# One transposition and one correction product for both tiles of a pair, and bias rows by label

## The reference, cut to what matters

```python
x = x + conv(x masked by length, one SSM kernel per channel)       # L0, a causal convolution, masked again
x = x + einsum('bct,bcd->bdt', x, weights[cond])                    # L1, mixing of channels, 16 sets
x = x + x @ base_weight.T + base_bias + (x @ A[id].T) @ Bw[id].T    # L2, 32 adapters of rank 16
x = x + x @ W.T + (x @ lora_A[label]) @ lora_B_w.T * 0.5            # L3, 5 labelers of rank 32
```

## Time and profile before

| | |
|---|---|
| time, median of 3 runs | 1446.25 us (1444.93 to 1446.51) |
| profiled execution: its own time | 1442.18 us |
| its span, first to last instruction | 1440.4 us |
| granted TensorE clock | 1.000 |
| PE busy | 1429.8 us, 99% |
| DVE busy | 1127.4 us, 78% |
| ACT busy | 612.7 us, 43% |
| POOL busy | 100.9 us, 7% |
| DMA | 271.94 MB, mean 189 GB/s |

### The profile page before, as it was taken

The page is one execution under the profiler, slowest core; times in us unless marked ns, Lnnn a source line. Parts: engine busy times, 40 slices in busy tenths (PEclk is TensorE's granted clock), DMA queues, the critical chain, the costliest instruction groups (busy, mean ns, idle before and its releaser), DMA issues.

```text
span 1440.4 us, 31629 instructions
## 1 busy us (share of the span) xinstructions
PE 1429.8 (99%) x9368; PEld 1329.8 (92%) x9368; DVE 1127.4 (78%) x2288; ACT 612.7 (43%) x1217; POOL 100.9 (7%) x193
## 2 busy tenths in 40 slices
PE   9999999999999999999999999999999999999998
PEld 7888899999999999999999999999999999999997
DVE  7975498888888887777777777787777777778775
ACT  4331376666666663333433433433343343343331
POOL 2322100000000002000000000000000000000000
PEclk9999999999999999999999999999999999999999
DMA  8033288888888886564564565556556556555652
GB/s 315 1 129 79 76 283 272 276 277 272 277 268 276 273 274 183 170 203 148 166 200 146 162 197 163 153 182 190 153 162 204 146 161 203 153 153 190 182 154 81
DMA packets 117070, 271.94 MB, mean 189 GB/s; under 512 B 24173, under 2 KB 60401, under 8 KB 114381
## 3 DMA queue, kind: packets, MB, share of 16 engines
q1 hardware_dynamic: 107048, 237.86, 54.1%
q10 hardware_dynamic: 9990, 33.68, 5.8%
HBM read 198.59 MB, written 72.85 MB: 188 GB/s over the span
## 4 chain that ended last, share of the span: by engine, by line
PE 95%; DVE 2%; DMA 2%; SPq 0%; issue 0%; POOL 0%; ACT 0%; DVEq 0%; POOLq 0%; ACTq 0%
PE ps L796 18%; PE ps L789 17%; PE ps L1704 14%; PE ps L788 12%; PE ps L769 8%; PE ps L1603 7%; PE ps L1715 6%; PE ps L805 4%; PE ps L1695 3%; PE ps L1707 2%; PE ps L1589 1%; PE ps L780 1%; PE ps L1612 1%; DMA p<-in_L_cond_base_weight 1%; DMA out<-y_out 1%; PE ps L775 1%
## 5 line engine op out<-in xcount | busy, mean ns | idle before, releaser
L789 PE MATMUL ps<-weights,xa 128*128 128x352 f32 x1152 | 323.0, 322 | 0.0
L788 PE MATMUL ps<-weights,xa 128*128 128x256 f32 x1152 | 321.8, 281 | 0.5 <-ACT y_out L597 0.5
L796 PE MATMUL ps<-weights,xs 128*128 128x512 f32 x1152 | 291.2, 401 | 0.0
L796 PEld LDWEIGHTS ps<-weights,xs 128*128 128x128 f32 x1152 | 207.0, 189 | 40.4
L1704 PE MATMUL ps<-toep,ut 128*128 128x512 f32 (+2 forms) x1152 | 226.7, 342 | 0.0
L788 PEld LDWEIGHTS ps<-weights,xa 128*128 128x128 f32 x1152 | 217.3, 189 | 2.5 <-issue 1.1
L789 PEld LDWEIGHTS ps<-weights,xa 128*128 128x128 f32 x1152 | 216.2, 188 | 1.3
L1704 PEld LDWEIGHTS ps<-toep,ut 128*128 128x128 f32 x1152 | 194.3, 189 | 16.6
L568 ACT ACTIVATE a<-ps 128x512 f32<-128x512 f32 x128 | 76.7, 599 | 281.9 <-PE ps L769 281.2
L769 PE MATMUL ps<-m_gath,x_in 128*128 128x128 f32 x1024 | 134.6, 275 | 1.3 <-DVE x_in L660 1.3
L769 PEld LDWEIGHTS ps<-m_gath,x_in 128*128 128x128 f32 x1024 | 126.6, 191 | 4.0 <-DVE x_in L660 1.5
(11 more groups left out here) (227 smaller groups left out, 2255.3 us busy)
## 6 DMA issues: line engine op xcount, KB each, us to landing
xt<-in_xt SPq DMA_DIRECT2D x64, 512.0 KB, 5.7
x_d<-yo SPq DMA_DIRECT2D x64, 512.0 KB, 2.9
x_nat<-in_x SPq DMA_DIRECT2D x64, 512.0 KB, 3.8
lags<-kern_d SPq DMA_DIRECT2D x63, 512.0 KB, 5.0
x_in<-x_d SPq DMA_DIRECT2D x62, 512.0 KB
out<-y_out ACTq DMA_DIRECT2D x62, 512.0 KB, 5.8
stack<-b_d SPq DMA_DIRECT2D x130, 128.0 KB, 3.9
tab<-a_d SPq DMA_DIRECT2D x128, 128.0 KB, 2.1
```

The costliest lines, as they stand in the source:

```text
L788: mm(acc[:, left, 0:HALF], x_part, w[:, 0:HALF], start=start, stop=end, skip_group_check=True)
L789: ins = mm(acc[:, right, 0:HALF + KR], x_part, w[:, HALF:WIDE], start=start, stop=end, skip_group_check=True)
L796: ins = mm(acc[:, bank], operand[:, a, i, :], plain(i, b, m), start=opens and i == a == b == 0, stop=i == K4 - 1 and a == 1, skip_group_ch ...
```

## The change: what it does

- `hrow`, `hc` and `c_gath` exist once and hold both tiles: rows and columns 0 to 79 are tile 0, and from 80 on for tile 1 in part. One `turn` and one `adapters` product serve a pair. The high half of `hs[1]` and `stack[1]` stands in the upper rows.
- The bias is no longer part of `c_gath`. The bias row with the correction of a label is made beforehand for each of the 5 labels (`row_d`, 5 x 2 x 1024) and loaded into the stack by label: one more DMA per sample.
- SP reads all eight ids (adapter and label of four samples) before it waits for `p_done` and loads the stacks, then the eight ids of the next pair.
- `low_rank(0, 0)` goes behind M3; `adapters` goes behind quarter 1; on VectorE `h_stack` of both tiles goes behind L738.
- In the preparation the bias product goes from "c" to "a3b", "c" gets five one-column products and "row" two more wide ones.

```diff
     def load_stack(eng, v, a, l):
         for b in range(2):
             row = b * (R2 + R3)
+            high, low, bias = HIGH[v] + row, LOW[v] + row, LOW[v] + 2 * b
...
+            eng.dma_start(f(stack[v][bias:bias + 2, 1]), row_d[bass.ds(l[b], 1)].squeeze(0)).then_inc(stack_landed[v], 16)
...
         def load_c(v, a, l):
             for b in range(2):
...
-                sp.dma_start(c_gath[v][rows, H3], c_adapters[bass.ds(a[b], 1), :, cols].squeeze(0)).then_inc(c_landed[v], 16)
-                sp.dma_start(c_gath[v][KS + b:KS + b + 1, H3], c_d[AR:AR + 1, cols]).then_inc(c_landed[v], 16)
+                row = v * KS + b * (R2 + R3)
+                to = c_gath[row:row + R2, v * KS + R2:v * KS + R2 + R3]
+                sp.dma_start(to, c_adapters[bass.ds(a[b], 1), :, bass.ds(l[b] * R3, R3)].squeeze(0)).then_inc(c_landed[v], 16)
...
         def stacks(n):
...
+            a, l = [ids(sp, n, v, B) for v in range(2)], [ids(sp, n, v, 2 * B) for v in range(2)]
             sp.wait_ge(p_done, n)
             for v in range(2):
-                load_stack(sp, v, ids(sp, n, v, B))
+                load_stack(sp, v, a[v], l[v])
...
@@ VectorE, pair(n)
             dve.wait_ge(m2_done, n + 1)
             h_rows(n, 0)
-            h_columns(n, 0)
             if not last_one:
                 choose(n + 1, 1, 0)
             dve.wait_ge(m4_done, n + 1)
             h_rows(n, 1)
-            h_stack(n, 0)
-            h_columns(n, 1)
             if not last_one:
                 first_low(n + 1)
+            h_columns(n)
+            if not last_one:
                 choose(n + 1, 1, 1)
-            h_stack(n, 1)
             dve.wait_ge(m6_done, n + 1)
             dve.wait_ge(pair_sums, 2 * n + 2)
             tt(y_out[0][:, HB:T], y_out[1][:, HB:T], of_p, ALU.add).then_inc(u2_read, 1)
+            for v in range(2):
+                h_stack(n, v)
...
@@ TensorE, pair(n)
-            wide_product(xa22, M4, V_LEFT, V_RIGHT, FRONT, False)
-            turn(n, 0)
-            wide_product(xa22, M4, V_LEFT, V_RIGHT, BACK, False).then_inc(m4_done, 1)
-            adapters(n, 0)
+            wide_product(xa22, M4, V_LEFT, V_RIGHT, ALL, False).then_inc(m4_done, 1)
...
             plain_product(xs2, M6, P_BANK, FRONT, True)
-            turn(n, 1)
+            turn(n)
             plain_product(xs2, M6, P_BANK, BACK, False).then_inc(m6_done, 1)
-            pe.wait_ge(hs_lo, 2 * n + 1)
-            pe.wait_ge(stack_landed[0], 64 * n + 64)
...
-            low_rank(0, 0, PIECES_S).then_inc(lr11_done, 1)
-            adapters(n, 1)
             if not last_one:
                 quarter(n + 1, 1)
+            adapters(n)
             pe.wait_ge(s4_lo, n + 1)
             ready(pe, y12_added, n)
             plain_product(xs4, M3, Q_BANK, ALL, True)
+            pe.wait_ge(hs_lo, 2 * n + 1)
+            pe.wait_ge(stack_landed[0], 96 * n + 96)
...
+            low_rank(0, 0, PIECES_S).then_inc(lr11_done, 1)
             if not last_one:
                 quarter(n + 1, 2)
...
@@ preparation: VectorE, then TensorE
+            dve.wait_ge(in_b3, 16)
+            ts(b3n[B3_ROWS], b3n[B3_ROWS], 0.5, None, ALU.mult).then_inc(b3_scaled, 1)
             t = target("c")
             dve.wait_ge(job_done, done("c"))
+            nc.vector.tensor_copy(crt[B3_ROWS], t[0:R3, HB + LR:HB + LR + L3N]).then_inc(crt_ready, 1)
...
-            over_chunks(t[0:1, HB + LR:HB + 2 * LR], lambda c: bias_col[:, c:c + 1], lambda c: a3raw[:, c, :]).then_inc(job_done, 1)
+            for l in range(L3N):
+                ins = mm(t[0:R3, HB + LR + l:HB + LR + l + 1], c_row[:, l * R3:(l + 1) * R3], ones[0:1, 0:1], start=True, stop=True)
+            ins.then_inc(job_done, 1)
             t = job("row")
             pe.wait_ge(bias_ready, 1)
+            pe.wait_ge(b3_scaled, 1)
```

More of the change, by code:

```diff
@@ L106, in program @@
     bias_col, o = at("bias_col", [P, K8], F32, o)
-    ones, o = at("ones", [P, 1], F32, o)
+    ones, o = at("ones", [P, L3N], F32, o)
+    crt, o = at("crt", [P, L3N], F32, o)
     o = o_w[0]
@@ L135, in program @@
     c_row, o = at("c_row", [1, LR], F32, o)
+    b3n, _ = at("b3n", [P, T], F32, o_c - AR // P * 4 * T)
     assert o <= o_w[2]
@@ L229, in program @@
     m_gath = both("m_gath", [P, P])
-    hrow = both("hrow", [P, P])
+    hrow = place("hrow", [P, P])
     x_nat[1], o = at("x_nat1", [P, T], F32, o_rest + 4 * T + 4 * TFOLD)
@@ L362, in program @@
     PAIRS = TILES // 2
-    c_adapters = c_d[0:AR].rearrange("(a r) c -> a r c", r=R2)
+    c_adapters = c_d.rearrange("(a r) c -> a r c", r=R2)
     x1_rows = x1_d.rearrange("(n b) c t -> n (b c) t", b=2)
@@ L484, in dense_sync @@
         for v in range(2):
-            for to, of in ((stack[v][H3], b3_d), (stack[v][KS + R2:KS + R2 + R3, 0], b3_d[:, 0]), (stack[v][KS:KS + 2, 1], row_d)):
+            high, low = HIGH[v] + R2, LOW[v] + R2
+            for to, of in ((stack[v][high:high + R3], b3_d), (stack[v][low:low + R3, 0], b3_d[:, 0])):
                 sp.dma_start(f(to), of).then_inc(rows_landed, 16)
@@ L770, in quarter, with turn, adapters @@
             ins.then_inc(mixed, 1)
[L772 to L780, removed]
+        def turn(n):
+            pe.wait_ge(hrow_ready, 2 * n + 2)
+            ready(pe, hc_ready, n)
+            nc.tensor.transpose(acc[:, SMALL_BANK, 0:P], hrow[:], ident[:]).then_inc(turned, 1)
+        def adapters(n):
+            for v in range(2):
+                pe.wait_ge(c_landed[v], 32 * n + 32)
+            pe.wait_ge(hc_ready, n + 1)
+            ready(pe, hs_lo, 2 * n)
+            mm(acc[:, SMALL_BANK, P:2 * P], c_gath[:], hc[:], start=True, stop=True).then_inc(adapted, 1)
         def wide_product(operand, m, left, right, chunks, opens):
@@ L800, in low_rank @@
         def low_rank(v, col, pieces):
-            for j, rows in ((0, P), (1, KS + 2)):
+            for j, rows in ((0, P), (1, (KS + 4, P)[v])):
                 at_col = col
@@ L1175, in _ @@
             act.wait_ge(staged_lo, 8)
-            act.wait_ge(c_stored, 32)
+            act.wait_ge(c_stored, 16)
+            act.wait_ge(split_const, 3)
             lower_high(1)
@@ L1664, in _ @@
                             lambda c: a3raw[:, c, :])
-            over_chunks(t[0:1, HB + LR:HB + 2 * LR], lambda c: bias_col[:, c:c + 1], lambda c: a3raw[:, c, :]).then_inc(job_done, 1)
+            for l in range(L3N):
+                ins = mm(t[0:R3, HB + LR + l:HB + LR + l + 1], c_row[:, l * R3:(l + 1) * R3], ones[0:1, 0:1], start=True, stop=True)
+            ins.then_inc(job_done, 1)
             t = job("row")
             pe.wait_ge(bias_ready, 1)
+            pe.wait_ge(b3_scaled, 1)
             for half in range(2):
                 cols = slice(half * HB, (half + 1) * HB)
-                ins = mm(t[0:1, cols], ones[:], b3t[:, cols], start=True, stop=True)
+                mm(t[0:L3N, cols], ones[:], b3t[:, cols], start=True, stop=False)
+            pe.wait_ge(crt_ready, 1)
+            for half in range(2):
+                cols = slice(half * HB, (half + 1) * HB)
+                ins = mm(t[0:L3N, cols], crt[B3_ROWS], b3n[B3_ROWS, cols], start=False, stop=True)
             ins.then_inc(job_done, 1)
```

125 lines of the change are left out of this document (59 added, 66 removed).

## The result

| | before | after |
|---|---|---|
| median of the timed runs (6 each) | 1445.29 us (1443.25 to 1446.51) | 1528.65 us (1524.64 to 1533.54) |
| ratio, 95% interval | | 1.0582 (1.0559 to 1.0604) |
| span of the profiled execution | 1440.4 us | 1526.8 us |

The change makes the kernel 5.8% slower. The forecast was 1528.0 us.

The account below looks back on a forecast made before the run. TensorE, 99% busy, bounded the kernel, with the chain through SP's queue nearly as long; 77 + 1.2 - 0.3 + 1 + 3 = 82 us on 1442.2 gave 1524, plus 4 for the timed median: 1528 us, range 1495 to 1560 us.

Parts of the forecast that it names:

- Part 1: On TensorE, one turn and one adapters product fewer save 0.34 us per pair, 11 us over 32 pairs.
- Part 2: Moving low_rank(0, 0) right before quarter 2 makes TensorE wait there for ScalarE's take, 1.5 us in 31 pairs.
- the SP loop: Quarter 3 through SP's loads, the tables and VectorE's u3_read to the next low_rank(1, HB): 27.1 + 4.5 = 31.6 us.
- Part 3: On the SP queue, four more id reads (2.6 us) and four row loads (1.9 us) per pair ahead of the tables.
- X: Time added to SP's list ahead of the table loads per pair: 4.5 us, taken from 3.6 to 5.5.
- the prediction's own signs of being wrong: Among them: third to eighth SP read after the x1 loads not at about 0.26 us.
- Rival 2: Id reads behind the x1 loads on SP all stay slow, X = 7.3: 149 us more, 1595 us; chance 0.08.
- Part 4: The pair's period is the mean of the SP loop, 31.6 us, and TensorE's own way, 28.8: 30.2 against 27.64.
- TensorE's own way: TensorE's period per pair without waits on SP's list: 27.64 - 0.34 + 1.5 = 28.8 us.
- Part 5: In the preparation, TensorE's added records, one-column products and wait for scaled b3n (0 to 2 us): together +3 us.
- Rival 1: SP's longer list stays hidden, only the wait at quarter 2 counts: 40 us more, 1486 us; chance 0.10.
- rival 3: No wait at quarter 2, SP's additions hidden, only TensorE's saving counts: -8 us, 1438 us; chance 0.04.

Follow-up runs that it names:

- run 10: Run 9 with the x1 load of tile 1 issued as soon as quarter 2 is mixed, tile 0's behind quarter 3: 1444.3 us, ratio 0.9997.
- Run 4: The kernel before, with only low_rank(0, 0) moved behind M3: 1549.4 us, ratio 1.072.
- run 5: The kernel before, with four more id reads (unused) on SP between stack and table loads in 29 pairs: 1487.4 us, ratio 1.0284.
- Run 9: run 1 plus low_rank(0, 0) mid-M3, b3_scaled wait behind the products with ones, SP's loop reordered, eight ids read once per pair: 1480.2 us, ratio 1.0249.
- run 2: The changed kernel, with SP reading the eight stack ids before it waits for the mixed quarters: 1613.3 us, ratio 1.1164.
- run 6: The changed kernel without the four row_d loads in pairs 1 to 31, their bias correction left out: 1533.9 us, ratio 1.0613.
- run 1: The changed kernel, with ScalarE taking quarter 1 before it waits for lr11_done and copies y11: 1498.4 us, ratio 1.0367.

## Why the prediction was right

The number was right by some luck. The sum was 82 us and the profiled execution took 1528.85 - 1442.18 = 86.7 us more. The 4 us that the forecast added for the median, as it stood above the profiled execution before, made up for the difference: in the changed kernel the median, 1528.65, is level with the profiled execution.

**Part 1** (-0.34 us). Right: in run 10 TensorE needs 19.38 us from M2's start to quarter 3, and 19.71 before, 0.33 less. It was worth its size only while nothing else made TensorE wait, as the prediction's first paragraph says.

**Part 2** (+1.5 us per pair at quarter 2). Right: 37.9 / 26 = 1.46 us. The consequences were not seen whole. The late product holds ScalarE's copy, and with it `take`, `h_high`, `h_low` and `u3_read`. The prediction followed only the `take`. Run 4 is the proof, with 3.5 us per pair from this one edit. In the changed kernel this third loop lies just below the SP loop, and so doesn't show in the number.

**Part 3** (X = 4.5 us). Somewhat high: from the x1 load to the first stack load SP took 1051.48 - 1043.31 = 8.17 us in the pair shown, 8.15 on average over the pairs (4.64 before), where 4.7 + 6 x 0.65 = 8.6 were forecast; from the first stack load to the last table load 1066.22 - 1051.48 = 14.74, against 14.14 before, as worked out (-1.3 + 1.9). Together X = 3.5 + 0.6 = 4.1 us, within the bounds of 3.6 and 5.5. The assumption on the slow reads was wrong as to which, and one of the prediction's own signs of being wrong came: not the first two reads are slow but two to four of the second to sixth. The medians of the third, fourth and fifth are 0.87, 1.07 and 0.57 us, not 0.26. They lie in a stretch of time behind the x1 loads. What they cost together is near what was assumed, so the term came out. Rival 2 (all slow) is false.

**Part 4** (period 30.2 us). Measured 30.32. That the mean of two loops decides is borne out by run 5; in the changed kernel itself it is not tested, since two lengths measured from one period always have it as their mean. But the terms are other ones. From 600 to 1400 us the period is 30.28 us and R comes 0.95 us late. So the SP loop was 30.28 + 0.95 = 31.23 us long, where 31.6 were forecast, and TensorE's own way 30.28 - 0.95 = 29.33, where 28.8 were. The first is 0.4 us shorter, as X is. The second is 0.5 us longer: 0.3 by the wait at M2, and the rest in small gaps behind the waits (0.13 us between quarters 2 and 3, 0.1 between R and M5). So two errors, about half a microsecond each, cancelled in the mean: one of them (X) was bounded in the prediction and the other not named.

The wait at M2 could have been read from the trace of before. There ScalarE's copies already waited for the store, 1.7 us per pair, with TensorE untouched:

```profile
ACT y_out L592 <- DMA out<-y_out: 48.5, 29, 2.1
```

The prediction counted what a late `u3_read` does to TensorE, and not to the store that is issued behind it.

**Part 5** (+3 us). Too small: the step in question is `b3_scaled` as a wait of "0 to 2 us". The job behind it starts at 113.58 us, 6.5 later than in the kernel before (107.05). The wait was 2.35 us, since VectorE's scaling took 2.62 us, where the scaling of as many numbers (L1478) took 0.68 in the kernel before; and the next four records took 3.37 instead of 1.88 at the lower clock. Run 9 takes 3.6 us of that back. The first R came 8.2 us late instead of 3 plus 1.2. That is 4 of the 4.7 us that the sum lacked.

**Rivals.** Rival 1 (SP hidden) falls by run 5 and by the wait for `u3_read` in every pair, rival 2 by the row of the eight reads, rival 3 by the wait at quarter 2 in every pair.

## What to carry to other kernels

An edit that makes one signal later must be followed through all its readers, and through what stands behind each of them in its engine's queue. Here one product moved by 3 us on TensorE reached `take`, the low halves of the weights, a sum, and at last an output store that then ran beside a large load. Taking work off the queue that seems to bound the loop can be worth nothing, or cost much (runs 2 and 6), when that work kept two transfers apart; look at the store's landing time in each trace. And where two loops alternate, a microsecond saved in one of them is worth half (run 1), and less once a third loop is near (run 6).

## What the runs showed of the hardware

- A 512 KB store took 4.6 to 4.9 us (median) with one of the x1 loads issued a quarter earlier (and 4.6 in run 1), 5.8 in the kernel before, 6.0 with the change, and 8.6 in run 2, where two 512 KB loads and twelve small ones were issued within 7 us of it.
- A register read from memory (TENSOR_LOAD) takes 0.26 us (median), but from 0.5 up to 1.9 us for one to four of those that fall some 1 to 6 us behind the issue of two 512 KB loads.
- After 2.35 us without work TensorE was granted 0.57 of its clock for 3.5 us.
- VectorE's scaling of 32 x 1024 floats took 2.62 us in the preparation of the changed kernel, and 0.68 in the kernel before:

```profile
110.09 0.68 DVE L1478 TENSOR_SCALAR b3t<-b3t 32x1024 f32<-32x1024 f32 x1 [1.73 <-DMA b3t<-in_L_cond_lora_B_w]
```

In the kernel before GpSimd was idle then. With the change GpSimd was at work as the scaling began (L1031, 2.34 us from 105.44 on), and the scaling ended 0.55 us after it, about the time that it takes by itself. That points to GpSimd as the reason; no run has taken it away.
